# Two mixture-of-experts stages of a vision tower on one Trainium2 core: GpSimd's sums in half pieces, routing steps and a share transpose at other places, unread products in the first tile, waits reordered at the stages' ends

## The reference

```python
# layer 0 (after a layer norm)
gate_scores = jnp.einsum('bsd,ed->bse', x, Wg) + bg
topk_scores, topk_idx = jax.lax.top_k(gate_scores, K)
topk_probs = jax.nn.softmax(topk_scores, axis=-1)
for e in range(E):
    h = jax.nn.relu(jnp.einsum('bsd,hd->bsh', x, W1[e]) + b1[e])
    y = jnp.einsum('bsh,dh->bsd', h, W2[e]) + b2[e]
    out = out + combine[..., e:e + 1] * y
# layer 1 (after an RMS norm)
for e in range(E):
    hh = jax.nn.silu(flat @ w1[e].T) * (flat @ w3[e].T)
    out = out + weights[:, e:e + 1] * (hh @ w2[e].T)
```

## Time and profile before

| | us |
|---|---|
| median of 3 runs (1112.57 to 1115.13) | 1114.5 |
| the profiled execution | 1118.76 |
| its span, first to last instruction | 1117.0 |
| PE busy (share of the span) | 1013.7 (91%) |
| DVE busy | 836.0 (75%) |
| ACT busy | 560.9 (50%) |
| POOL busy | 388.1 (35%) |

### The profile page before, as it was taken

The page is one execution under the profiler, slowest core; times in us unless marked ns, Lnnn a source line. Parts: engine busy times, 40 slices in busy tenths (PEclk is TensorE's granted clock), DMA queues, the critical chain, the costliest instruction groups (busy, mean ns, idle before and its releaser), DMA issues. The chain is left out here.

```text
span 1117.0 us, 23308 instructions
## 1 busy us (share of the span) xinstructions
PE 1013.7 (91%) x8383; PEld 726.3 (65%) x8383; DVE 836.0 (75%) x2034; ACT 560.9 (50%) x1279; POOL 388.1 (35%) x319
## 2 busy tenths in 40 slices
PE   6897889789999999997998889988999999999997
PEld 2475756566666666664675567764777777777774
DVE  1786959877877787776677589965877777787875
ACT  2375646565454555554237757764544444444441
POOL 3234402303333333323238477720033333333332
PEclk9999999989999999999998999999999999999999
DMA  8300000022223222232001000000112122211112
GB/s 220 137 1 2 2 1 2 1 48 49 48 58 85 52 49 49 67 78 49 1 19 37 19 1 3 3 2 1 49 54 56 57 71 76 63 55 55 54 55 66
DMA packets 76422, 50.16 MB, mean 45 GB/s; under 512 B 4196, under 2 KB 75124, under 8 KB 75924
## 3 DMA queue, kind: packets, MB, share of 16 engines
q1 hardware_dynamic: 75972, 44.59, 15.6%
q0 software_dynamic: 336, 4.07, 0.9%
HBM read 45.99 MB, written 2.66 MB: 44 GB/s over the span
## 5 line engine op out<-in xcount | busy, mean ns | idle before, releaser
L1576 PE MATMUL moe_psU<-moe_nT_parts,moe_w_hi 128*128 128x320 f32 x988 | 320.9, 336 | 24.4 <-DVE moe_hid L1486 17.1
L1576 PE MATMUL moe_psU<-moe_nT_parts,moe_w_lo 128*128 128x320 f32 x988 | 295.2, 309 | 0.0
L1576 PEld LDWEIGHTS moe_psU<-moe_nT_parts,moe_w_hi 128*128 128x128 f32 x988 | 186.8, 189 | 80.4 <-issue 41.6
L1218 ACT ACTIVATE moe_silu<-moe_psU 128x320 f32<-128x320 f32 x286 | 123.9, 439 | 141.3 <-PE moe_psU L1576 122.8
L1223 ACT ACTIVATE moe_hid<-moe_psU,middle 128x320 f32<-128x320 f32 x260 | 130.7, 526 | 116.0 <-PE moe_psU L1576 112.4
L1576 PEld LDWEIGHTS moe_psU<-moe_nT_parts,moe_w_lo 128*128 128x128 f32 x988 | 187.4, 190 | 0.0
L1480 DVE TENSOR_TENSOR moe_hid<-moe_psU,moe_silu 128x320 f32<-128x320 f32 x286 | 131.3, 485 | 34.8 <-ACT moe_silu L1218 28.0
L1110 POOL TENSOR_TENSOR moe_y_sum<-moe_y_sum,moe_y 128x640 f32<-128x640 f32 x48 | 74.8, 1558 | 150.6 <-DVE moe_y L1441 84.0
L1591 PE MATMUL moe_psY<-moe_hid,middle 128*64 128x320 f32 x800 | 120.0, 442 | 3.6 <-DVE moe_y L1441 3.0
L1591 PE MATMUL moe_psY<-moe_hid,late 128*64 128x320 f32 x800 | 118.7, 439 | 0.9 <-DVE moe_hid L1480 0.9
L1486 DVE TENSOR_SCALAR moe_hid<-moe_psU,middle 128x320 f32<-128x320 f32 x156 | 84.1, 547 | 31.4 <-PE moe_psU L1576 26.6
(11 more groups left out here) (367 smaller groups left out, 1905.3 us busy)
## 6 DMA issues: line engine op xcount, KB each, us to landing
moe_share<-shares SPq DMA_DIRECT2D x208, 160.0 KB, 4.5
images<-in_x SPq DMA_DIRECT2D x8, 576.0 KB, 11.8
late<-in_late POOLq DMA_DIRECT2D x1, 2263.5 KB, 11.3
out_tokens<-h SPq DMA_DIRECT2D x13, 160.0 KB, 1.8
middle<-in_middle POOLq DMA_DIRECT2D x1, 1554.0 KB, 7.1
project_turns<-in_turns SPq DMA_DIRECT2D x8, 160.0 KB, 2.2
early<-in_early SPq DMA_DIRECT2D x1, 1043.0 KB, 19.8
turns_first<-in_turns SPq DMA_DIRECT2D x4, 160.0 KB, 2.2
```

What stands on the lines that cost most here:

```text
L1218: act.activation(sil[bank][:, :], psU[u % 2][:, 0:HALF], ACT.Silu).then_inc(hid_act, 1)
L1576: last = pe.matmul(psum[:, 0:HALF], w[:, col:col + SPLIT], moving, start=(part == 0), stop=(part == 1))
```

## The change

POOL's `add_pairs` adds the same operands in two halves of 320 columns, six instructions for three; `summed` is counted at the second half. In layer 0 the slots of the routing and norm steps are moved: the two norm steps `nn` of (1, 1) go to (1, 0) and (1, 2), two of the seven `a` of (1, 4) go to (1, 7), `aaa` of (2, 0) goes to (2, 1), behind that place's eviction, and ACT's exponential goes from (2, 1) to (2, 3). In layer 1 the transpose of the shares goes from (2, 3) to (3, 0). ACT issues `parts_ahead` before the last `read_out`. `down(12, 0)` waits for the evictions of its own pair and no longer for the tile's last unit. In layer 0's first tile PE issues one unread product at (0, 4), (1, 4) and (2, 4), where other tiles have a `down`.

```diff
--- before.py
+++ after.py
@@ -1075,14 +1075,14 @@
             OUTS, READS = [(1, 0)], [(1, 1)]
             SHARES, SHARES_READ = (2, 6), (2, 7)
             TURN, KEEP = [(3, 2)], [(3, 2)]
-            HI, EXP = (1, 5), (2, 1)
+            HI, EXP = (1, 5), (2, 3)
             NORM_STEPS, ASK_STEPS, END_STEPS = 5, TOP_TWO_LINKS + 1, 5
             LAST_SLOTS = {(0, 7): "ss", (1, 1): "sssss", (1, 7): "sssss", (2, 1): "mmm", (2, 7): "mmm", (3, 3): "s"}
-            SLOTS = {(0, 4): "aaaannnn", (1, 1): "nn", (1, 4): "aaaaaaan", (2, 0): "aaa", (2, 4): "neeeeee"}
+            SLOTS = {(0, 4): "aaaannnn", (1, 0): "n", (1, 2): "n", (1, 4): "aaaaan", (1, 7): "aa", (2, 1): "aaa", (2, 4): "neeeeee"}
         else:
             LOGITS, DOWN = (0, 0), 1
             OUTS, READS = [(1, 0), (1, 3)], [(1, 1), (1, 4)]
-            SHARES, SHARES_READ = (2, 3), (3, 0)
+            SHARES, SHARES_READ = (3, 0), (3, 0)
             TURN, KEEP = [(3, 1), (3, 3)], [(3, 1), (3, 3)]
             HI, EXP = (1, 3), (0, 3)
             NORM_STEPS, ASK_STEPS, END_STEPS = 2, 2, 18
@@ -1102,12 +1102,14 @@
                 def add_pairs(j):
 
                     need(pool, out_mm, j * PARTS)
-                    pool.wait_ge(weighed, j * PAIRS + 2)
-                    pool.tensor_tensor(y_sum[:, :], y[:, 0, :], y[:, 1, :], ALU.add).then_inc(summed, 1)
-                    for p in (2, 3):
-                        pool.wait_ge(summed, j * SUMS + (p - 1))
+                    for p in (1, 2, 3):
                         pool.wait_ge(weighed, j * PAIRS + (p + 1))
-                        pool.tensor_tensor(y_sum[:, :], y_sum[:, :], y[:, p, :], ALU.add).then_inc(summed, 1)
+                        need(pool, summed, (j * SUMS + (p - 1)) if p > 1 else 0)
+                        for half in range(2):
+                            cols = slice(half * HALF, half * HALF + HALF)
+                            into, before = y_sum[:, cols], (y_sum if p > 1 else y[:, 0, :])[:, cols]
+                            ins = pool.tensor_tensor(into, before, y[:, p, cols], ALU.add)
+                        ins.then_inc(summed, 1)
 
                 def add_first(j):
 
@@ -1298,10 +1300,11 @@
                     high_weights(p)
                 over_bodies(body)
                 body(NT - 1)
+                if ahead:
+                    parts_ahead()
                 for part in range(PARTS):
                     read_out(NT - 2, part)
                 if ahead:
-                    parts_ahead()
                     tables_ahead()
 
             @block.vector
@@ -1581,7 +1584,7 @@
                         need(pe, weighed, j * PAIRS + (p - 1) if p > 1 else 0)
                     else:
                         need(pe, weighed, j * PAIRS + (p - 1 if last and p else p))
-                    last_unit = UPG - 1 if last else first_of[p] + 2 * len(chunks[p]) - 1
+                    last_unit = UPG - 1 if last and p else first_of[p] + 2 * len(chunks[p]) - 1
                     wait_evicted(pe, j, last_unit)
                     if layer == 0:
                         wait_evicted(pe, j, max(u for u in range(last_unit) if on_dve[u] != on_dve[last_unit]))
@@ -1642,6 +1645,8 @@
                             logits(g)
                         if g and k == DOWN:
                             down(g - 1, p)
+                        elif layer == 0 and k == DOWN and p < 3:
+                            products_unread(pe, psY_both[:, 0:512], early, ec, 1)
                         for part in range(PARTS):
                             if g >= 2 and (p, k) == OUTS[part]:
                                 turn_out(g - 2, part)
```

## The result

The changed kernel takes 1102.57 us (median of 5 executions, 1096.56 to 1106.21) against 1114.5 us: a ratio of 0.9897, 95% interval 0.9858 to 0.9936. A second series of five executions gave 1098.22 us (1096.64 to 1103.37) against 1115.16, ratio 0.9851 (0.9825 to 0.9876). By these medians it is 1.0 to 1.5% faster; the forecast was 1103.2.

The account below looks back on a forecast made before the run. PE, busy for 91% of the span, bounds the kernel, with waits for DVE's evictions in the expert stages. Terms sum to -11.35 us, taken off the median of 1114.5: 1103.2 us, own range 1100.5 to 1106 (with rivals 1098 to 1111.5).

Parts of the forecast that it names:

- layer 0, ten middle tiles: Layer 0's middle tiles: earlier weighing removes PE's 1.15 us wait, 0.36 returns at the transpose; 0.79 a tile, -7.9 us.
- layer 0, second tile's steps: Layer 0's second tile: L930 and L931 now meet POOL's adds with no time won ahead; +0.5 us (0 to 0.7).
- first tile, clock: Layer 0's first tile: unread products fill PE's idle time and may keep its clock at 2.4 GHz; -0.7 us.
- layer 0, last tile: Layer 0's last tile: the same steps move past each other with POOL silent; 0 us.
- layer 0, end: Layer 0's end: earlier parts let PE run through, gain 4.7, less 0.8 waiting for POOL's sum; -3.9 us.
- layer 1, middle tiles: Layer 1's middle tiles: PE's wait moves to psU3, POOL's halves slow DVE 0.2 us a tile; +2.0 us.
- layer 1, first tile: Layer 1's first tile: four products fit into 0.72 us of PE's idle time; -0.5 us.
- layer 1, end: Layer 1's end: `down(12, 0)` no longer waits 0.85 us; -0.85 us.
- Rival 1: Layer 0's middle tiles: DVE gets the port between halves, 0.44 us more in ten tiles, 1098.8 us; chance 0.12.
- Rivals 2 and 4: Layer 0's middle tiles: 2, no gain, weighing 0.8 us late, 1111.1, chance 0.14; 4, halves slow DVE, 1116.1, 0.08.
- The halves' size: POOL's adds: a pair of halves takes 1.84 us instead of 1.56; 72 adds grow 14 us in sum.
- Rival 3: Layer 0's end: only a third of the gain, L1388 held longer, weighing late for psY; 1106 to 1107, chance 0.11.

Follow-up runs that it names:

- the old places: Changed kernel with layer 0's routing and norm steps and exponential put back where they stood before: 1110.62 us, ratio to before 0.9957.
- the run with whole adds: Changed kernel with each POOL sum again one add of 640 columns instead of two halves: 1099.88 us, ratio to before 0.9861.
- the old ends: Changed kernel with its edits at the ends of both expert stages taken back: 1109.24 us, ratio to before 0.9929.
- both together: Changed kernel, whole adds, `add_up` between sums, layer 1's store behind share transfers, layer 0's first sum held to the third weighing: 1087.12 us, ratio to before 0.9726.
- the order that avoids it, with the store behind: Changed kernel, `add_up` between second and third sum, layer 1's store behind the share transfers; with halves kept 1096.38 us, ratio to before 0.9786.

## Why the prediction was right

The total (1103.2 against 1102.57 and 1098.22; at equal clock -12.6 us against -11.35) is right, and so is the mechanism in each stage. That the total is this close is in part luck: nearly every term gained more than forecast, and the largest miss the other way, layer 0's end, makes up for some of it. Term by term, measured as differences between transposes or waits in the timelines of one execution each:

| term | predicted | measured |
|---|---|---|
| layer 0, ten middle tiles | -7.9 | -8.5 |
| layer 0, second tile's steps | +0.5 | +0.1 |
| first tile, clock | -0.7 | -1.3 to -1.9 |
| layer 0, last tile | 0 | -0.5 |
| layer 0, end | -3.9 | -4.1 |
| layer 1, middle tiles | +2.0 | +0.9 |
| layer 1, first tile | -0.5 | -0.6 |
| layer 1, end | -0.85 | -0.9 |

The right-hand column adds up to some -15 and not to -12.6, and the difference is clock. The first tile's term is clock altogether, and equal clock takes it out. Of layer 0's end 1.0 to 1.3 us is clock as well: before, a stretch of 3.4 us at 0.50 lies inside that end (from 530.71), and in the changed kernel it lies behind `turn_out(12)`, from 528.97. Counted to the recurrence's products behind it (547.91 before, 532.36 after), the end gains 2.8 to 3.1 us and not 4.1. Without these two the terms add up to some -12.4.

**Middle tiles of layer 0.** Each step came: the norm held by the first of `add_up`'s two (forecast to end 0.33 us behind it, it was 0.35), the weighing directly behind its `down`, L930 and L931 held by one half each. From the weighing's start to the last weights it was to be 5.97 us and is 5.90 (405.24 to 411.14). The wait at (2, 2) was to give back 1.15 us and gave 1.08, and the transpose was to lose 0.36 and loses 0.22, which makes 0.87 a tile instead of 0.79. **Rival 1** fell, but not because GpSimd takes the port from a DVE instruction that waits: L930 waited at the change of halves and ended 0.10 us after the second half had started. L931 starts 0.13 us too late in each of the eleven tiles in which it meets the halves, and is held for 0.80 us. The halves alone changed the total in neither order. **Rivals 2 and 4** hung on the weighing's start, which was at 405.24 and not 0.8 us later or at its old place.

**The halves' size** was one mis-sized term: a pair takes 1.71 us, not 1.84, as the second half starts before the first one's end by the trace. GpSimd's busy time grew by 11.6 us (388.1 to 399.7), not 14. So the second tile lost 0.1 and not 0.5 us (19.35 against 19.23 with the old places), layer 1's L1337 took 0.58 and not 0.69 us, and its tile grew by 0.09 and not 0.2.

**The clock** was a term with a wide bound, and it came near its good end. In before's profile 6.83 us stood at 0.50, in the changed one none, and the tile after the first transpose went from 21.18 to 19.35 us. The kernel without the products gives them 1.3 us of that.

**Layer 0's end** was right for its reason: DVE's L1391 start at 508.96 without waiting for `turn_out(11)`, the weighing frees psY at 513.4, and 14.2 us became 9.35 (forecast 9.5). The -3.9 took the long `down` (3.71 us instead of 2.37) as gained, but it was a half-clock stretch that only moved behind the end, so 2.8 to 3.1 us remain. The wait for GpSimd's sum that was to cost 0.8 us costs 0.71 by the run with whole adds. **Rival 3**, a third of the gain, is out: the old ends cost 3.3 to 3.6 us here with that stretch left out. Missed was the last tile, priced at 0 because GpSimd is silent there; it is 0.54 us shorter, and with the old places 23.66 us again, so the order of the steps counts without any hold.

**Layer 1** went as written, with the wait moved from the transpose to psU3. The prediction took DVE's queue there as given. What it did not ask is which of DVE's steps GpSimd held in it: `add_up`'s adds held routing steps between the second and third weighing (L1418 for 0.89 us, where the same step takes 0.18 with both together), and the order that avoids it, with the store behind, was worth 0.9 us a tile, as much as the change gained in a tile of layer 0.

## What to carry to other kernels

When two engines hold each other up and only one of them sets the tile's length, the order of the other's instructions is a free parameter: put them where the first has steps that are not stretched (here its reductions and its reads of PSUM) or nothing to do, and ask of each moved step which queue waits for its result. Here GpSimd's order was worth as much again as the whole change (13.3 us at equal clock against 12.6), but only once a store that waited for it no longer stood ahead of transfers on SyncE's queue. A half-clock stretch that moves from one part into the next makes a part look faster: count to an instruction behind it. And compare executions at equal clock before you split a few microseconds between edits.
